# Graph attention pass: POOL's messages in two instructions, and a landing wait ahead of every fourth gather

## The reference, cut to what matters

```
score = einsum('ehd,ehd->eh', K[src], Q[dst]) / sqrt(HD) + edge_bias     # 8 heads of 32
m     = segment_max(score, dst)
ex    = exp(score - m[dst]);  denom = segment_sum(ex, dst)
out   = segment_sum((ex / denom[dst])[:, :, None] * V[src], dst)
```

## Time and profile before

| | us |
|---|---|
| median of 3 runs | 5461.48 (5446.13 to 5467.12) |
| profiled execution, its own time | 5467.72 |
| its span from first to last instruction | 5465.8 |
| PE busy in the span | 3936.6 (72%) |
| DVE busy | 3067.4 (56%) |
| POOL busy | 2451.9 (45%) |

### The profile page before, as it was taken

How to read it: one execution, slowest core, us unless ns; L and a number is a source line. 1 busy time by engine, 2 the same in 40 slices (tenths; PEclk the granted TensorE clock), 3 DMA queues, 4 the chain that set the end, 5 groups by cost and what they waited for, 6 DMA issues and landing times. The chain is left out here.

```text
span 5465.8 us, 69110 instructions
## 1 busy us (share of the span) xinstructions
PE 3936.6 (72%) x16154; PEld 2869.7 (53%) x16282; DVE 3067.4 (56%) x7623; ACT 1863.3 (34%) x5073; POOL 2451.9 (45%) x2442
## 2 busy tenths in 40 slices
PE   6867777767777659966953666666666328999999
PEld 4545545555555448866732444444444226777776
DVE  3277778877778775662063666666667773111111
ACT  1333333333333313311222444444445322333332
POOL 2256566666556360000166666666663321333332
PEclk8978888888888879987986767777777559999999
DMA  2545555555555332221173333333332360111111
GB/s 83 185 135 147 142 148 148 147 149 148 142 147 144 89 109 86 94 64 38 44 254 91 93 92 94 94 92 90 91 94 57 113 204 18 33 31 31 31 32 27
DMA packets 316126, 553.64 MB, mean 101 GB/s; under 512 B 63430, under 2 KB 213782, under 8 KB 315856
## 3 DMA queue, kind: packets, MB, share of 16 engines
q0 software_dynamic: 137120, 388.63, 26.6%
q1 hardware_dynamic: 178736, 161.98, 9.6%
HBM read 459.75 MB, written 90.62 MB: 101 GB/s over the span
## 5 line engine op out<-in xcount | busy, mean ns | idle before, releaser
L427 POOL DMA_INDIRECT attend_ring<-kv_rows,all_step_src x880 | 855.5, 972 | 669.8 <-PE attend_ps_agg L468 415.6
L927 POOL DMA_INDIRECT edge_ring<-head_rows,all_step_src x880 | 871.5, 990 | 485.9 <-issue 213.5
L963 PE MATMUL edge_ps_agg<-edge_msg,edge_sel 128*128 128x264 f32 x1760 | 670.7, 520 | 168.8 <-issue 67.9
L468 PE MATMUL attend_ps_agg<-attend_msg,attend_sel 128*128 128x264 f32 x1760 | 620.0, 456 | 179.3 <-DVE graph_qa L781 127.5
L963 PEld LDWEIGHTS edge_ps_agg<-edge_msg,edge_sel 128*128 128x128 f32 x1760 | 420.3, 259 | 292.6 <-issue 161.4
L452 PE MATMUL attend_ps_q<-graph_qa,attend_sel_t 128*128 x1760 | 538.9, 436 | 29.1 <-ACT attend_sel_t L577 23.2
L1256 DVE TENSOR_TENSOR graph_acc<-graph_acc,edge_ps_agg 128x264 f32 x880 | 369.5, 420 | 338.8 <-PE edge_ps_agg L963 166.2
L2811 DVE TENSOR_TENSOR moe_gl<-moe_ps_h,moe_act 128x341 f32<-128x341 f32 x210 | 107.9, 514 | 776.8 <-PE moe_ps_h L2729 776.8
L781 DVE SCALAR_TENSOR_TENSOR graph_qa<-graph_qa,all_step_same,attend_ps_agg 128x264 f32 x880 | 421.6, 479 | 190.8 <-remote 138.3
L468 PEld LDWEIGHTS attend_ps_agg<-attend_msg,attend_sel 128*128 128x128 f32 x1760 | 333.6, 213 | 350.9 <-issue 155.6
L2729 PE MATMUL moe_ps_h<-experts_w,moe_xt 128*128 x1680 | 501.8, 451 | 0.6 <-ACT moe_xt L2760 0.6
(11 more groups left out here) (424 smaller groups left out, 6404.4 us busy)
## 6 DMA issues: line engine op xcount, KB each, us to landing
attend_ring<-kv_rows,all_step_src POOLq DMA_INDIRECT x880
edge_ring<-head_rows,all_step_src POOLq DMA_INDIRECT x880
kv_rows<-qkv_kv SPq DMA_DIRECT2D x25, 512.0 KB, 3.0
experts_w<-in_w_t SPq DMA_DIRECT2D x16, 682.0 KB
attend_mask<-run_starts SPq DMA_DIRECT2D x440, 8.1 KB
edge_mask<-run_starts SPq DMA_DIRECT2D x440, 8.1 KB
head_rows<-hds_hh SPq DMA_DIRECT2D x25, 264.0 KB
qkv_x<-in_x SPq DMA_DIRECT2D x25, 256.0 KB, 3.2
```

The costliest lines, as they stand in the source:

```text
L427: nc.gpsimd.indirect_dma_start(ring[:, step % RING1, :], None, g.kv_rows, bass.IndirectOffsetOnAxis(g.step_src[:, step:step + 1], 0)).then ...
L468: nc.tensor.matmul(ps_agg[i % SUM_BANKS][:, 0:AGG], sel[:, q % 2, u % QU, :], msg[:, q % 2, u % QU, :], start=True, stop=True).then_inc(s_ ...
L927: nc.gpsimd.indirect_dma_start(ring[:, n % slots, u, :], None, g.head_rows, bass.IndirectOffsetOnAxis(g.step_src[:, step:step + 1], 0)).th ...
L963: nc.tensor.matmul(ps_agg[i % BANKS][:, 0:AGG], sel[:, q % 2, u % QU, :], msg[:, q % 2, u % QU, :], start=True, stop=True).then_inc(s_agg, 1)
```

## The change

POOL's message instruction is cut in two, of two steps each. The first stands where the whole one stood and makes the messages of steps 12 and 13; the second makes those of 14 and 15, and stands after the gathers of offsets 8, 9 and 10, ahead of that of offset 11. PE waits for the first at step 12 and for the second at step 14. ACT's wait counts both. And each gather whose step is a multiple of four (offsets 0, 4, 8, 12), from the 45th gather on, waits, besides the sum, until all four gathers of the group before it have landed.

```diff
-            def last_messages(b):
+            def last_message(b, i):
 
-                k = b * quarters + quarters - 1
-                pool.wait_ge(landed[k % groups], (k // groups + 1) * (16 * QU))
-                pool.wait_ge(s_msg, (b + 1) * PAIRS_DVE)
-                pool.wait_ge(s_agg, (k - 1) * QU)
-                first = k * QU % RING1
-                nc.gpsimd.tensor_tensor(msg[:, 1].rearrange("p u (h c) -> p u h c", c=HC)[:, :, :, 0:HD],
-                                        ring[:, first:first + QU, D:2 * D].rearrange("p u (h d) -> p u h d", h=H),
-                                        prob[:, b % 2].rearrange("p h u -> p u h")[:, CH - QU:CH, :].unsqueeze(3)
-                                        .to_broadcast([P, QU, H, HD]), ALU.mult).then_inc(s_pool_msg, 1)
+                k, u = b * quarters + quarters - 1, CH - QU + i
+                if i == 0:
+                    pool.wait_ge(landed[k % groups], (k // groups + 1) * (16 * QU))
+                    pool.wait_ge(s_msg, (b + 1) * PAIRS_DVE)
+                    pool.wait_ge(s_agg, (k - 1) * QU)
+                first = (b * CH + u) % RING1
+                nc.gpsimd.tensor_tensor(msg[:, 1, i:i + 2].rearrange("p u (h c) -> p u h c", c=HC)[:, :, :, 0:HD],
+                                        ring[:, first:first + 2, D:2 * D].rearrange("p u (h d) -> p u h d", h=H),
+                                        prob[:, b % 2].rearrange("p h u -> p u h")[:, u:u + 2, :].unsqueeze(3)
+                                        .to_broadcast([P, 2, H, HD]), ALU.mult).then_inc(s_pool_msg, 1)
 
             for step in range(count * CH + RING1):
-                if step >= RING1 and (step - RING1) % CH == CH // 2:
-                    last_messages((step - RING1) // CH)
+                if step >= RING1 and (step - RING1) % CH in (CH // 2, CH // 2 + 3):
+                    last_message((step - RING1) // CH, (step - RING1) % CH // (CH // 2 + 1) * 2)
...
                 if step >= RING1:
                     pool.wait_ge(s_agg, step - RING1 + 1)
+                    if step % QU == 0:
+                        before = step // QU - 1
+                        pool.wait_ge(landed[before % groups], (before // groups + 1) * (16 * QU))
...
-                    if u == CH - QU:
-                        pe.wait_ge(s_pool_msg, b + 1)
+                    if u >= CH - QU and u % 2 == 0:
+                        pe.wait_ge(s_pool_msg, b * 2 + (u - (CH - QU)) // 2 + 1)
...
-                    act.wait_ge(s_pool_msg, a - 1)
+                    act.wait_ge(s_pool_msg, (a - 1) * 2)
```

## The result

The changed kernel takes 5718.28 us (5711.32 to 5728.0, 4 runs) against 5454.98 (5446.13 to 5467.12, 4 runs): ratio 1.0469, interval 1.0450 to 1.0489. That is 263 us slower. The forecast had the sign right and said 5503; the range ended at 5552.

The account below looks back on a forecast made before the run. The PE-DVE chain bounds the attention pass at 29.47 us a turn, no engine saturated. POOL's new period of 30.25 adds 0.78 us over 52 turns, 41 us: 5461.5 + 41 = 5503, range 5450 to 5552.

Parts of the forecast that it names:

- The split, 0 to 0.2 us a turn: POOL's message cut in two in the attention pass: alone it costs 0 to 0.2 us, taken as 0.
- 0.85 a turn for the second half: In POOL's period, between the gathers of offsets 10 and 11: 0.99 us less 0.14 for a gather following a message sooner.
- The landing wait gives POOL's list a period that binds: Four landing waits a turn set a period the pass can't go below: 30.25 us against 29.47, +0.78 a turn.
- The form of the sum: POOL's period per turn: 4 x (3.75 + R) + 0.85 = 15.85 + 4R, forecast at 30.25 us.
- R: Time from the start of a group's last gather to the next group's first, landing wait deciding: 3.6 us, 3.3 to 3.8.
- The issue at 1.25 us: POOL's gathers within a group: three issue steps of 1.25 us, 3.75 us a group, four groups a turn.
- Rival 1: Chain through PE and POOL, via the second half at step 14, slower than forecast: 31.2 us a turn, +70 us; chance 0.16.
- Rival 2: PE's stall between steps 14 and 15 goes; if R is under 3.40, faster, 55 us gained at 3.14; chance 0.15.
- Rival 3: Nothing seen: R about 3.4, POOL's new period equals the old turn, within 0.5% of before; chance 0.23.
- The upper end of +82 us: Outer end of the loss in the attention pass, with R at 3.8 and a period of 31.05 us.

## Why the prediction was right or wrong

**The split, 0 to 0.2 us a turn.** Alone it costs nothing: 0.9953, a gain of 26 us. A half takes 1.08 us, not 0.99. Beside the four waits it does cost: the turn is 34.4 against 34.0 us and the ratio 1.0469 against 1.0407. The forecast had 0.85 a turn for the second half in POOL's period.

**The landing wait gives POOL's list a period that binds.** Right, and it is nearly the whole loss: 1.0407 with the waits alone, and 0.9915 for the changed kernel when they move by one gather. The form of the sum was right too: its terms, measured, add up to the turn.

**R = 3.6, kept between 3.3 and 3.8.** This is the step that failed. R came out at 4.44 in the mean (4.17 to 4.56 by offset). The traffic was read rightly: 3.32 us were taken and 3.33 measured. But to it I added 0.28 us, which a gather takes after a release by PE's sum, and one sentence, that the semaphore may come "a little" after the last byte, for which the sum had nothing. Measured, 1.10 us pass between the last packet and the next gather: 0.38 until the landing wait ends and 0.72 until the gather starts, because this wait is an instruction of its own. With the waits swapped it is 0.60. Each 0.1 us of R is worth 0.4 us a turn and 21 us of time, and my band for R was 0.5 wide around a reading that left out one part. Four R of 17.75 in place of 14.4 are 3.35 of the 4.15 us a turn that were missed.

**The issue at 1.25 us.** The other eleven steps take 14.45 us in place of 13.75. Of 382 gathers ahead of them 39 take more than 1.0 us (the one of 1042.44 took 1.62), and their mean is 0.99 against the usual 0.95; eight times POOL idles 1.4 us before such a step. Why these are longer stays open. The second half costs 0.1 more than forecast. With this the sum closes: 30.25 + 3.35 + 0.70 + 0.11 = 34.4.

**Rival 1**, in which PE waits at step 14 for the second half, came true as a sign (2.75 us at 1022.01) of the same period, not as a chain of its own. **Rival 2** was right in its mechanism: the stall went, and its point of decision, R under 3.40, was the right test. R was a full microsecond above it, so POOL's period took back all and more of what PE gained. **Rival 3** is refuted.

**The range.** It took its ends from R and from nothing else. The upper end of +82 us was computed with all other terms at their best values. The sign came out right for the reason given, but only the size of R separated this forecast from rivals 2 and 3, and R was the term that was wrong.

## What to carry to other kernels

A wait for a DMA's landing in the list of the engine that issues the DMAs makes a period of its own. Count it from issue to the next issue, with the time from the last byte to the start of the released instruction, which was 1.1 us here (0.6 where the instruction carried the wait itself); and do so before asking which engine is on the critical path. Where a run of transfers has to be thinned out, a delay of fixed length (1.66 us between gathers in place of 1.25) was worth 2.15%; waits for landings, with R in them, gave 1.8% at best and cost 4.7% with four of them in the wrong places. A wait's place within a group is worth as much as its presence: one gather later, and with the two waits swapped, a loss of 4.7% became a gain of 0.85%.

## What the runs showed of the hardware that I had not expected

PE falls behind its own records while POOL issues gathers of 256 KB about every 1.25 us for eight and more in a row, though nothing that its next instruction waits for is missing: the sum of step 15 needs DVE's `add` of step 13, which in the turn of the earlier trace rows ended at 1010.94. In 44 turns of the kernel before, from 400 to 1700 us, DVE starts on the sum of step 15 between 1.0 and 4.1 us after the end of PE's record; in the changed kernel it is 0.15 us. It shows as remote waits of DVE, 2.7 us a turn, at whatever place of PE's list the run's end falls: the last `add` in the kernel before, L707 with the split. At 1.66 us between gathers it goes. DVE's remote waits also go in the changed kernel, though ACT's at L581 stay there (76.5 us, 21 times); with one landing wait a turn DVE's shrink.

A slower clock is not what holds PE up. In the kernel before, PE has no record from 1012.96 to 1016.40, and the windows around that time (columns as above) show the clock at full until DVE's wait is over at 1015.22; it falls at 1015.4:

```profile
1012.00:1014.00 2.00, 0.96 (x6) 0.76 (x4) 0.46 (x2) 0.00 (x0) 1.51 (x2) 1.00 0.71 223
1014.00:1016.00 2.00, 0.00 (x0) 0.00 (x0) 0.53 (x2) 0.89 (x3) 1.39 (x3) 0.85 0.73 215
1016.00:1018.00 2.00, 1.17 (x3) 0.81 (x4) 1.46 (x3) 1.31 (x5) 0.88 (x1) 0.50 0.74 205
1018.00:1020.00 2.00, 2.00 (x6) 1.56 (x5) 1.30 (x4) 0.00 (x0) 0.94 (x1) 0.50 0.28 104
```

So the stall costs more than the wait that shows it: at the lower level the four matmul records of a query (L452) take 1.91 us at 1019.19, against 1.03 at 1009.84. What PE lacks in the stall stays open; no run took the traffic away and kept the issue, or the other way round.

The wait that an indirect DMA of POOL carries is released faster than one that stands ahead of it as an instruction. From the last semaphore update of the landing to the gather's start, the trace has 0.26 us in the first case and 0.76 in the second.
